# Graph attention on one core: reciprocals of the row sums turned by DMA through DRAM instead of by TensorE and ScalarE

## The reference, cut to what matters

```
h = relu(layernorm(x))
q, k, v = h @ Wq + bq, h @ Wk + bk, h @ Wv + bv          # per head: 1024 x 32
scores = q @ k.T / sqrt(32) + (1 - adj) * -1e9           # 1024 x 1024 per head
attn = softmax(scores)                                   # over the keys
out = x + (attn @ v) @ Wo + bo
```

## Time and profile before

| | before |
|---|---|
| median of 3 runs | 1139.5 us |
| time of the profiled execution | 1138.54 us |
| its span, first to last instruction | 1136.6 us |
| busy: TensorE (matmul) | 1101.3 us, 97% |
| busy: ScalarE | 1019.7 us, 90% |
| busy: VectorE | 964.0 us, 85% |
| busy: GpSimd | 131.5 us, 12% |
| mean granted TensorE clock | 0.991 of full speed |

### The profile page before, as it was taken

The page is one execution under the profiler, slowest core; times in us unless marked ns, Lnnn a source line. Parts: engine busy times, 40 slices in busy tenths (PEclk is TensorE's granted clock), DMA queues, the critical chain, the costliest instruction groups (busy, mean ns, idle before and its releaser), DMA issues.

```text
span 1136.6 us, 28159 instructions
## 1 busy us (share of the span) xinstructions
PE 1101.3 (97%) x10756; PEld 894.8 (79%) x10756; DVE 964.0 (85%) x1747; ACT 1019.7 (90%) x1883; POOL 131.5 (12%) x234
## 2 busy tenths in 40 slices
PE   5599999999999999999999999999999999999997
PEld 4378888888878878888887878878887887878775
DVE  4599889988899888998889978898889988888875
ACT  2499999999999999999999999999999999999995
POOL 3102000021000210021001200012000021000001
PEclk9699999999999999999999999999999999999999
DMA  8532242423423243332423324242242323223101
GB/s 276 154 94 58 60 125 64 106 59 79 127 62 94 55 120 93 76 93 56 124 75 86 94 57 129 60 105 73 71 124 59 103 57 97 72 73 90 45 20 38
DMA packets 76596, 99.51 MB, mean 88 GB/s; under 512 B 17968, under 2 KB 43696, under 8 KB 76464
## 3 DMA queue, kind: packets, MB, share of 16 engines
q1 hardware_dynamic: 75504, 95.10, 31.6%
q0 software_dynamic: 576, 1.57, 0.6%
q10 hardware_dynamic: 384, 1.05, 0.3%
HBM read 22.15 MB, written 8.39 MB: 27 GB/s over the span
## 4 chain that ended last, share of the span: by engine, by line
PE 90%; ACT 6%; DVE 1%; ACTq 1%; issue 1%; DMA 1%; POOL 0%; DVEq 0%
PE ps_turn L693 29%; PE ps_scores L679 22%; PE ps_heads L756 18%; PE ps_side L700 9%; PE ps_side L727 5%; PE ps_side L709 5%; ACT rows L439 3%; ACT turned_a L444 1%; ACTq L278 1%; PE ps_turn L700 1%; PE ps_heads L716 1%; PE ps_heads L742 1%; ACT turned_b L449 0%; DMA xn<-in_x 0%; DVE rows L529 0%
## 5 line engine op out<-in xcount | busy, mean ns | idle before, releaser
L529 DVE CUSTOM_DVE_ANT_0 rows<-ps_scores,mask 128x1024 f32<-128x1024 f32 x512 | 613.0, 1215 | 32.0 <-issue 23.7
L439 ACT ACTIVATE rows<-rows,row_min 128x1024 f32<-128x1024 f32 x512 | 587.2, 1150 | 17.7 <-DVE row_min L529 17.4
L693 PE MATMUL ps_turn<-ident_r,rows_raw 128*128 128x128 f32 x4096 | 462.9, 256 | 6.6 <-ACT turned_a L444 4.9
L693 PEld LDWEIGHTS ps_turn<-ident_r,rows_raw 128*128 128x128 f32 x4096 | 399.0, 141 | 74.0 <-issue 35.5
L444 ACT ACTIVATE turned_a<-ps_turn 128x512 f32<-128x512 f32 x512 | 305.5, 597 | 52.1 <-PE ps_turn L693 52.0
L679 PE MATMUL ps_scores<-k_stack,q_stack 128*128 128x512 f32 x1024 | 317.5, 422 | 12.8 <-DMA k_stack<-start_k_lo 12.1
L536 DVE COPY turned_b<-ps_turn 128x512 f32<-128x512 f32 x328 | 225.6, 688 | 35.8 <-PE ps_turn L693 27.1
L679 PEld LDWEIGHTS ps_scores<-k_stack,q_stack 128*128 128x128 f32 x1024 | 167.1, 189 | 35.8 <-issue 14.8
L417 POOL COPY inv_wide<-row_inv 128x256 f32<-128x256 f32 x64 | 25.5, 399 | 943.9 <-DVE row_inv L564 916.1
L756 PE MATMUL ps_heads<-turned_a,v 128*32 128x256 f32 x2048 | 123.8, 382 | 0.6 <-ACT inv_wide L474 0.6
L756 PE MATMUL ps_heads<-turned_b,v 128*32 128x256 f32 x2048 | 122.2, 379 | 0.0
(11 more groups left out here) (59 smaller groups left out, 567.0 us busy)
## 6 DMA issues: line engine op xcount, KB each, us to landing
q_stack<-q_hi SPq DMA_DIRECT2D x240, 64.0 KB, 2.0
q_stack<-q_lo SPq DMA_DIRECT2D x240, 64.0 KB, 2.0
k_stack<-k_hi SPq DMA_DIRECT2D x240, 64.0 KB, 2.0
k_stack<-k_lo SPq DMA_DIRECT2D x240, 64.0 KB, 2.0
res<-in_x SPq DMA_DIRECT2D x32, 256.0 KB, 2.7
out<-res SPq DMA_DIRECT2D x32, 256.0 KB, 2.5
xn<-in_x SPq DMA_DIRECT2D x7, 1024.0 KB, 6.1
mask<-in_adj SPq DMA_DIRECT2D x1, 3584.0 KB, 14.8
```

The lines of the kernel that those rows point to most:

```text
L439: nc.scalar.activation(rows[:, k, :], rows[:, k, :], ACT.Exp, bias=row_min[:, k:k + 1], scale=-1.0, accum_out=row_sum[:, u % 2, j:j + 1]). ...
L529: nc.vector.tensor_tensor_reduce(out=rows[:, k, :], in0=ps_scores[n % 2][:], in1=mask[:, qt, :], scale=1.0, scalar=START_MIN, op0=ALU.add, ...
L693: tr = nc.tensor.transpose(ps_turn[half][:, k, :].bitcast(F32R), rows_raw[:, n % RING, kt * P:(kt + 1) * P], ident_r[:])
```

## The change

The reciprocals no longer pass through GpSimd's copy, TensorE and ScalarE. GpSimd writes the 128 x 8 reciprocals, transposed, into a small DRAM tensor `inv_rows` (8 x 128; its runs are single 4-byte values), waits for that, and reads it back with four DMAs, each of which repeats 2 rows of 128 values over the 32 partitions of a head (`inv_t`, 128 x 2 x 128). `norm_heads` waits for these four. `invert` is moved one row earlier (`INV_ROW` 7 to 6), `norm_heads` one row later and to the end of the slot (`NORM_ROW` 1 to 2). `heads` waits for `heads_normed` itself now. The tables of the order by row and the places of the side work are new throughout.

```
-SCORES_AHEAD = (4, 5, 4, 4, 5, 4, 4, 5)
-MASK_AHEAD = (4, 4, 4, 3, 3, 3, 3, 3)
-EXP_AHEAD = (3, 2, 2, 2, 2, 2, 2, 1)
+SCORES_AHEAD = (4, 4, 4, 4, 5, 4, 4, 5)
+MASK_AHEAD = (4, 4, 3, 3, 3, 3, 3, 3)
+EXP_AHEAD = (1, 3, 2, 2, 2, 2, 2, 1)
...
-EXP_AT = (2, 2, 0, 0, 2, 2, 2, 0)
+EXP_AT = (0, 0, 0, 0, 0, 0, 2, 0)
...
-INV_ROW, NORM_ROW = 7, 1
+INV_ROW, NORM_ROW = 6, 2
...
-    (("qk", 0, (2, 2, 3, 3)), ("qk", 1, (5, 5, 5, 6)), ("o", 2, (10, 10, 11, 11)), ("qk", 2, (13, 13, 14, 14)),
+    (("qk", 0, (2, 2, 3, 3)), ("qk", 1, (5, 5, 6, 6)), ("o", 2, (9, 10, 11, 11)), ("qk", 2, (13, 13, 14, 14)),
...
-HT_ROWS = {(0, 28): 0, (0, 30): 1, (1, 1): 2, (1, 4): 3}
+HT_ROWS = {(0, 29): 0, (0, 30): 1, (1, 4): 2, (1, 6): 3}
...
 ACT_COPIES = (
-    (2, 3, 4, 11, 13, 18, 21, 24, 27, 30),
-    (0, 3, 6, 8, 10, 11, 13, 16, 19, 21, 24, 27, 29),
+    (2, 5, 6, 10, 13, 14, 17, 18, 21, 22, 26, 28, 29),
+    (0, 1, 2, 10, 13, 14, 18, 21, 22, 26, 29, 30),
 )
...
-        inv_wide, inv_wide_raw = sb_raw("inv_wide", [P, UNIT_ROWS, HEAD_DIM])
-        inv_t = inv_wide[:].rearrange("p j d -> p (j d)")
+        inv_rows = nc.dram_tensor("inv_rows", (UNIT_ROWS, P), F32, kind="Internal").ap()
+        inv_t = sb("inv_t", [P, UNIT_TILES, P])
...
-            def spread(b, g, u):
-                pool.wait_ge(inv_done, unit(b, g, u) + 1)
-
-                pool.wait_ge(inv_turned, unit(b, g, u) + START)
-                pool.tensor_copy(inv_wide[:], row_inv[:].unsqueeze(2).to_broadcast([P, UNIT_ROWS, HEAD_DIM])
-                                 ).then_inc(inv_spread, 1)
+            def turn_inv(b, g, u):
+
+                k = unit(b, g, u)
+                pool.wait_ge(inv_done, k + 1)
+                if k:
+
+                    pool.wait_ge(inv_in, k * PARTS * 16)
+                pool.dma_start(inv_rows.rearrange("j q -> q j"), row_inv[:], allow_slow_non_contiguous=True
+                               ).then_inc(inv_out, 16)
+                pool.wait_ge(inv_out, (k + 1) * 16)
+                if k:
+
+                    pool.wait_ge(heads_normed, k)
+                for h in range(PARTS):
+                    pool.dma_start(inv_t[h * HEAD_DIM:(h + 1) * HEAD_DIM, :, :],
+                                   inv_rows.rearrange("(t h) q -> h t q", h=PARTS)[h].partition_broadcast(HEAD_DIM)
+                                   ).then_inc(inv_in, 16)
...
-            def copy_inv(k):
-                act.wait_ge(inv_turned, k + 1 + START)
-                nc.scalar.activation(inv_t, ps_heads[:, UNIT_Q:], ACT.Copy).then_inc(inv_copied, 1)
...
             def norm_heads(k, g, u):
-                dve.wait_ge(inv_copied, k + 1)
+                dve.wait_ge(inv_in, (k + 1) * PARTS * 16)
                 dve.wait_ge(heads_done, k + 1)
...
-            def turn_inv(b, g, u, first, last):
...
             def heads(k, parity, g, half):
 
                 pe.wait_ge((copied_a, copied_b)[half], (k + 1) * UNIT_ROWS + START)
-                if half == 0:
+                if half == 0 and k:
 
-                    pe.wait_ge(inv_copied, k + 1)
+                    pe.wait_ge(heads_normed, k)
```

More of the change, by code:

```diff
@@ L27 @@
 RING = 4
-SCORES_AHEAD = (4, 5, 4, 4, 5, 4, 4, 5)
-MASK_AHEAD = (4, 4, 4, 3, 3, 3, 3, 3)
-EXP_AHEAD = (3, 2, 2, 2, 2, 2, 2, 1)
-EXP_AT = (2, 2, 0, 0, 2, 2, 2, 0)
-HIGH_AT = (0, 1, 1, 0, 0, 0, 1, 2)
-COPY_AT = (0, 0, 0, 1, 1, 1, 1, 1)
-TAKE_AT = (0, 1, 1, 0, 1, 0, 2, 2)
+SCORES_AHEAD = (4, 4, 4, 4, 5, 4, 4, 5)
+MASK_AHEAD = (4, 4, 3, 3, 3, 3, 3, 3)
+EXP_AHEAD = (1, 3, 2, 2, 2, 2, 2, 1)
+EXP_AT = (0, 0, 0, 0, 0, 0, 2, 0)
+HIGH_AT = (1, 1, 0, 0, 1, 2, 0, 2)
+COPY_AT = (1, 0, 0, 1, 1, 1, 1, 1)
+TAKE_AT = (2, 1, 1, 0, 2, 2, 0, 2)
 EPS = 1e-5
@@ L209, in gnn_kernel @@
         inv_done = sem("inv_done")
-        inv_spread = sem("inv_spread")
-        inv_turned = sem("inv_turned")
-        inv_copied = sem("inv_copied")
+        inv_out = sem("inv_out")
+        inv_in = sem("inv_in")
         heads_normed = sem("heads_normed")
@@ L494, in slot @@
                 pb, pg, kind, s = step_ended(b, g, i)
-                if r == 0 and not (first and i == 0):
-                    copy_inv(unit(b, g, i // UNIT_ROWS) - 1)
                 if kind == "qk" and HIGH_AT[r] == 0:
@@ L501, in slot @@
                         exp(m)
-                if (g, i - 1) in HT_ROWS and not last:
-                    copy_ht(b + 1, HT_ROWS[g, i - 1])
+                row_before = (g, i - 1) if i else (0, ROWS - 1)
+                if row_before in HT_ROWS and not last and (g or i):
+                    copy_ht(b + 1, HT_ROWS[row_before])
                 if kind == "qk" and HIGH_AT[r] == 1:
@@ L518, in _ @@
             slots(slot)
-            copy_inv(BATCH * BATCH_UNITS - 1)
         @block.vector
@@ L561, in invert @@
                 if not (first and u == 0):
-                    dve.wait_ge(inv_spread, unit(b, g, u))
+                    dve.wait_ge(inv_out, unit(b, g, u) * 16)
                 nc.vector.reciprocal(row_inv[:], row_sum[:, u % 2, :]).then_inc(inv_done, 1)
             def norm_heads(k, g, u):
-                dve.wait_ge(inv_copied, k + 1)
+                dve.wait_ge(inv_in, (k + 1) * PARTS * 16)
                 dve.wait_ge(heads_done, k + 1)
                 dst = heads_t[0][:, u * UNIT_Q:(u + 1) * UNIT_Q] if g == 0 else heads_t[1][:, u % 2, :]
-                nc.vector.tensor_tensor(dst, ps_heads[:, 0:UNIT_Q], inv_t, ALU.mult
+                nc.vector.tensor_tensor(dst, ps_heads[:, 0:UNIT_Q], inv_t[:].rearrange("p t q -> p (t q)"), ALU.mult
                                         ).then_inc(heads_normed, 1)
@@ L617, in slot @@
                 ended = step_ended(b, g, i)
-                if r == NORM_ROW and not (first and u == 0):
-                    norm_heads(unit(b, g, u) - 1, *((g, u - 1) if u else (1 - g, UNITS - 1)))
                 if r == INV_ROW:
@@ L633, in slot @@
                     take(*ended)
+                if r == NORM_ROW and not (first and u == 0):
+                    norm_heads(unit(b, g, u) - 1, *((g, u - 1) if u else (1 - g, UNITS - 1)))
                 for t in range(TILES):
@@ L730, in project_out @@
                     mm.then_inc(o_done, 1)
-            def turn_inv(b, g, u, first, last):
-                k = unit(b, g, u)
-                pe.wait_ge(inv_spread, k + 1)
-                if not (first and u == 0):
-                    pe.wait_ge(heads_normed, k)
-                if (g, u) in HT_UNITS and not last:
-                    pe.wait_ge(ht_done, (b + 1) * HT_STEPS + HT_UNITS[g, u])
-                for t in range(UNIT_TILES):
-                    tr = nc.tensor.transpose(ps_heads[:, UNIT_Q + t * P:UNIT_Q + (t + 1) * P].bitcast(F32R),
-                                             inv_wide_raw[:, t * PARTS:(t + 1) * PARTS].rearrange("p h d -> p (h d)"),
-                                             ident_r[:])
-                tr.then_inc(inv_turned, 1)
             def heads(k, parity, g, half):
                 pe.wait_ge((copied_a, copied_b)[half], (k + 1) * UNIT_ROWS + START)
-                if half == 0:
-                    pe.wait_ge(inv_copied, k + 1)
+                if half == 0 and k:
+                    pe.wait_ge(heads_normed, k)
+                    b, gu = k // BATCH_UNITS, (k // UNITS % PHASES, k % UNITS)
+                    if gu in HT_UNITS and b < BATCH - 1:
+                        pe.wait_ge(ht_done, (b + 1) * HT_STEPS + HT_UNITS[gu])
                 for kt in range(PARTS):
@@ L801, in slot @@
                         heads(unit(b, g, u) - 1, u + 1, g if u else 1 - g, half)
-                if r == INV_ROW:
-                    turn_inv(b, g, u, first, last)
                 if (g, i) in HT_ROWS and not last:
```

5 lines of the change are left out of this document (2 added, 3 removed), and 6 rows, old and new, of the table STEPS.

## The result

The changed kernel takes **1405.4 us** (median of 4 runs, 1401.3 to 1411.3), beside 1139.5 us before (4 runs): a ratio of 1.234, 95% interval 1.230 to 1.238. The profiled execution took 1406.5 us, its span is 1404.7. Forecast were 1132 us, in a range of 1121 to 1148. The direction was that of the third rival.

The account below looks back on a forecast made before the run. TensorE's own work was taken to bound the middle, with ScalarE also mattering in the last 56 us; -10.2 + 0 + 0 + 2.9 = -7.3 us gave 1132 us, range 1121 to 1148.

Parts of the forecast that it names:

- third rival: DRAM chain longer than its cover, from 11.7 us on: VectorE's multiplication waits every unit; 1210 to 1900 us; chance 0.22.
- The chain's length: RECIPROCAL through GpSimd's write and four reads to VectorE's multiplication: 9.2 us, bounds 6.7 to 24.4, costing 0 in the middle.
- The rule that spoke against the change: Skill's rule on GpSimd's write: one descriptor per element, 1024 in all, so time would go toward a chain outlasting its cover.
- the pair: Two transposes per unit removed from TensorE: 0.16 us each unit, -10.2 us over 64 units, bounds -7.7 and -20.5.
- the new lay of the side work: On TensorE, fewer side groups behind transposes (-4.2 us) and more runs of scores (+3.8 us) cancel: 0.
- ScalarE and VectorE stayed hidden: ScalarE net -1.9 us per batch of 136, VectorE gives copies away; both remain hidden behind TensorE.
- the normalisation of x on GpSimd: GpSimd's five DMAs are issued before it begins; over 4 us of air before TensorE's turn: 0.
- The cover: Time from RECIPROCAL to multiplication in the middle that hides the DRAM chain: up to about 11.6 us.
- The tail: In the last unit nothing hides the DRAM chain, so the multiplication comes later: +2.9 us, bounds +0.4 to +5.3.
- The two-port collision: VectorE's operations hold GpSimd's DMA issuing, up to 1.2 us five times: chain 15.3 us, about 1340 us; chance 0.03.

Follow-up runs that it names:

- experiment 1: The changed kernel with the multiplication using the previous unit's reciprocals from a doubled tile, so it no longer waits for the current reads: 1292.1 us.
- experiment 7: The kernel before, TensorE path kept, plus GpSimd's dense write of each unit's reciprocals in 1024 runs of 4 bytes, which nobody reads: 1366.1 us.

## Why the prediction was wrong, by its steps

**The chain's length: the step that failed.** The prediction put it at 9.2 us, `0.25 + 2.5 + 2.0 + 2.4 + 2.0`, and hidden up to 11.6. In the unit shown it is 15.6: 0.5 to hand over, 0.91 to issue (not 2.5), 10.2 for the landing and GpSimd's start behind it (not 2.0), 2.1 for four reads issued (2.4 right), and 1.9 from the last of them to the multiplication (2.0 right). Over all 64 units the median is 15.3. Landing is the term that was mis-sized, five times over. I had bounded the issue widely, from 0.49 to 15.7, and the landing hardly at all, 2.0 to 2.5, by rows of other transfers. The row that I took as the nearest, the load of 256 single values in 5.0 us, showed small runs in a **read** of DRAM, scattered over the partitions of SBUF; "for the DMA engines tiny runs are cheap" does not follow from it for a write. The change **writes** them to DRAM, side by side. Nothing in the trace of before had a small write in it; the honest bound from above was open.

**The rule that spoke against the change.** The write was slow. The Trainium skill (DMA: Bandwidth & Descriptors, Rules for kernel authors) advises against such a write, because a non-contiguous last dimension becomes one descriptor per element. But their number isn't the mechanism here: with 1024 runs at 64 B distance the kernel takes 1140.3 us, and a unit's write lands in 2.7 us; with half the runs, dense, 1388.5. The measurement decides: the number of small runs is not what cost, their adjacency was.

**The third rival was right in its place, near in its arithmetic, wrong in its condition.** It put the loss at "chain + 4.9 us" for a unit: 15.6 + 4.9 = 20.5, against 21 measured; and 1210 us at 13 us and 60 more for each further us give 1366 at 15.6, against 1405. That the sums come near is in part luck: the multiplication's wait, taken away alone, brought back only 113 of 266 us (experiment 1). Its condition, an issue over 5 us, did not come true, and I had set its chance (0.22) by that condition alone.

**What no case held.** The write costs time of engines that don't wait for it: 227 us in the kernel before, where nothing depends on it (experiment 7). In the change the two don't add: taking the multiplication's wait away brought 113 us and left 153 (experiment 1). And the clock: before, it stood at 1.00 in the middle, so no case had a price for the gaps beyond their own length.

**Right, by the run with contiguous writes** (1129.9 us, one execution; forecast 1132): TensorE is busy for 1092.4 us instead of 1101.3, -8.9, where I had -10.2 from the pair and 0 from the new lay of the side work; only their sum is tested. ScalarE and VectorE stayed hidden, and the normalisation of x on GpSimd cost nothing that shows. The cover was 10.8 us there (445.21 to 455.97), not 11.6, which is also why a unit of the change takes 21 us: 15.3 and the 5.8 that are left of 16.6. **The tail was wrong**: it was forecast at +2.9 for a chain of 9.2 us, and cost nothing. In the last unit of this run the multiplication waits 2.83 us for TensorE's product and not for the reads; it comes 8.6 us earlier than before (1122.23 against 1130.81), and the whole span is 8.5 us shorter. So the sum came near with a saving a little too large and a tail that wasn't there. **The two-port collision**, which I had left at 0.03: every issue of the write is between 0.907 and 0.990 us, every read's between 0.539 and 0.567, so VectorE never held GpSimd up.

**Range and chances.** The range stopped where the third rival began, with 0.22 left outside. Given an unmeasured kind of transfer on a path with 2.4 us of air, that was too little.

## What to carry to other kernels

Before costing a DMA, look for a row that has the same direction, size of run and neighbourhood at its destination; without one, leave its landing open, not only its issue, and count on side effects for others. A transposition by a DMA of 4-byte runs into dense DRAM is to be avoided even for 4 KB; turn the values on VectorE in one operation, then write long runs in one DMA. If such a write can't be avoided, space the values out: 64 B between them took the collision away here. And where small numbers must travel from one engine to the others, count DMAs as well as bytes: with four writes of half a microsecond each the version with one transposition took 1141.3 us, with one write 1135.8, on either side of the kernel before.

## What was unexpected of the hardware

- 1024 writes of 4 bytes to adjacent DRAM addresses: 9.3 us of wait behind the issue, 8.8 for 512 of them, 4.1 at 8 B distance, 2.7 at 64 B, 1.8 for contiguous runs of 32 B. The packets themselves are as quick dense as apart; the wait comes behind them.
- In that time other DMAs' copies come late, and engines stand still which have nothing to do with the transfer, up to 7.3 us at a time (experiment 1); a kernel that doesn't use the result loses 227 us in 64 such writes.
- GpSimd issues 1024 runs in 0.91 us, 128 runs of 32 B in 0.58, 8 runs in 0.52: some 0.4 ns per run of 4 B on top of half a microsecond, not 15. It isn't the number of runs alone: 128 runs of 128 B take 0.72.
- A transposition of 32 x 32 on VectorE takes 0.200 us and one of 128 x 32 0.211: four blocks cost as much as one.
- Behind a gap of TensorE of 3.4 us the granted clock fell to 0.50, and was back some 3.4 us later (the rows at 616 to 626 above).
